# Reordering the tail of a graph network's first layer: masks, joins, degrees and a weight split moved to earlier places on each engine

## The reference

```python
h = relu(layernorm(x)); x = x + L0(h)   # mean over incoming edges @ W_l.T + b_l + h @ W_r.T, relu
h = relu(layernorm(x)); x = x + L1(h)   # transformer: 4 blocks, attention over the edges,
                                        # layer norms scaled by a conditioning vector of each node
h = relu(layernorm(x)); x = x + L2(h)   # weighted graph convolution, one weight for each edge
h = relu(layernorm(x)); x = x + L3(h)   # edge network: mish(mish(edge_feat @ W1) @ W2), summed to nodes
```

```python
ph = noise_levels * freqs
emb = concatenate([sin(ph), cos(ph)])
cond = silu(emb @ f_w1 + f_b1) @ f_w2 + f_b2
scale, bias = cond @ sw + sb, cond @ bw + bb
```

## Time and profile before

| | us |
|---|---|
| median of 3 runs | 1599.44 (1599.12 to 1599.72) |
| profiled execution, its own time | 1600.61 |
| span of the profiled execution | 1597.4 |
| PE busy | 1511.4 (95%) |
| DVE busy | 1187.2 (74%) |
| ACT busy | 1076.7 (67%) |
| POOL busy | 649.0 (41%) |

### The profile page before, as it was taken

How to read it: one execution, slowest core, us unless ns; L and a number is a source line. 1 busy time by engine, 2 the same in 40 slices (tenths; PEclk the granted TensorE clock), 3 DMA queues, 4 the chain that set the end, 5 groups by cost and what they waited for, 6 DMA issues and landing times. The chain is left out here.

```text
span 1597.4 us, 26151 instructions
## 1 busy us (share of the span) xinstructions
PE 1511.4 (95%) x9086; PEld 1216.4 (76%) x9086; DVE 1187.2 (74%) x2049; ACT 1076.7 (67%) x1557; POOL 649.0 (41%) x471
## 2 busy tenths in 40 slices
PE   4998899999999999999999999999999999999987
PEld 4765587778787878787864578888888888888874
DVE  8995647564656465646634399999999999999967
ACT  8844536543654465445532289999999999999953
POOL 3430200110012001200300677888888888888501
PEclk9999899999999999999999999999999999999989
DMA  3002320013002300120104777777777777777610
GB/s 110 1 2 87 93 86 27 7 51 116 27 7 61 105 27 7 54 93 27 69 27 140 178 158 151 154 157 151 157 151 158 153 157 153 157 154 155 159 34 33
DMA packets 88590, 151.47 MB, mean 95 GB/s; under 512 B 23611, under 2 KB 28603, under 8 KB 88003
## 3 DMA queue, kind: packets, MB, share of 16 engines
q0 software_dynamic: 54400, 85.33, 27.2%
q1 hardware_dynamic: 34114, 65.15, 12.7%
HBM read 141.02 MB, written 9.31 MB: 94 GB/s over the span
## 5 line engine op out<-in xcount | busy, mean ns | idle before, releaser
L1876 POOL DMA_INDIRECT edge_gathered<-dst_table,edge_index x158 | 272.1, 1722 | 59.1 <-issue 37.2
L227 PE MATMUL edge_z2p<-edge_w_hi,edge_h_hi 128*128 128x512 f32 x628 | 252.3, 402 | 0.6 <-DVE edge_late L2243 0.6
L227 PE MATMUL edge_z2p<-edge_w_hi,edge_h_lo 128*128 128x512 f32 x628 | 247.9, 395 | 0.0
L227 PE MATMUL edge_z2p<-edge_w_lo,edge_h_hi 128*128 128x512 f32 x628 | 247.6, 394 | 0.0
L1848 POOL DMA_INDIRECT edge_gathered<-src_table,edge_index x158 | 175.1, 1108 | 83.8 <-issue 79.8
L1079 POOL TENSOR_TENSOR h<-h,tr_row_b 128x512 f32<-128x512 f32 x40 | 59.2, 1513 | 271.5 <-ACT C L1325 271.1
L1068 POOL TENSOR_TENSOR tr_cw<-w_c,tr_cw 32x1024 fp32r<-32x1024 f32 x7 | 16.6, 2372 | 318.8 <-ACT tr_cw L1285 318.8
L227 PEld LDWEIGHTS edge_z2p<-edge_w_hi,edge_h_hi 128*128 128x128 f32 x628 | 118.3, 188 | 32.5 <-issue 7.7
L227 PEld LDWEIGHTS edge_z2p<-edge_w_hi,edge_h_lo 128*128 128x128 f32 x628 | 118.2, 188 | 27.9
L227 PEld LDWEIGHTS edge_z2p<-edge_w_lo,edge_h_hi 128*128 128x128 f32 x628 | 118.3, 188 | 24.2
L1095 PE MATMUL tr_one<-tr_yT_hi,tr_w_hi 128*128 128x256 f32 (+2 forms) x384 | 119.3, 311 | 4.2 <-issue 4.2
(11 more groups left out here) (380 smaller groups left out, 3964.5 us busy)
## 6 DMA issues: line engine op xcount, KB each, us to landing
w_c<-in_attr_T SPq DMA_DIRECT2D x78, 128.0 KB
w_a<-in_wv SPq DMA_DIRECT2D x4, 1024.0 KB, 5.4
w_b<-in_wq SPq DMA_DIRECT2D x4, 1024.0 KB, 5.2
w_a<-in_wk SPq DMA_DIRECT2D x4, 1024.0 KB, 7.5
w_b<-in_wo SPq DMA_DIRECT2D x4, 1024.0 KB, 6.9
w_a<-in_m SPq DMA_DIRECT2D x4, 1024.0 KB, 5.2
w_b<-in_m SPq DMA_DIRECT2D x4, 1024.0 KB, 5.3
w_c<-in_cond_w SPq DMA_DIRECT2D x4, 768.0 KB, 5.5
```

What stands on the lines that cost most here:

```text
L227: mm = pe.matmul(out, a, b, start=(n == 0), stop=(n == last))
L1876: pool.indirect_dma_start(out=from_rows[ring][:, j, :].bitcast(F32), out_offset=None, in_=k.dst_table, in_offset=bass.IndirectOffsetOnAxis ...
```

## The change

In the tail of `front` the same work is put in another order, and one piece of the transformer's start is moved into it. On PE, `degT` goes from behind the two `cond` products to behind the fifth aggregate (`AGG` is indexed by `AHEAD` = 4). In the ring `beside` it then has the bank of the first `hidden`, and the two `cond` products come after it. On VectorE, the five joins and the first four masks go ahead of the taking of `hidden`, the fifth mask behind it, and the reciprocal of the degrees ahead of `cond`. On ACT, four sums of counts and four aggregates come ahead of the exponential. The first half of the weight split is made at the end of this tail, into a tile `first_parts` that lives through the whole program; the edge layer uses the same bytes as the first of its two `h1_lo` tiles. `ph` and `turns` become names for other tiles.

```diff
+        plan.add(("agg",) + AGG[AHEAD], "sca")
+        plan.add(("degT", 0), "vec", "beside")
+        for m, f in AGG[AHEAD + 1:]:
             plan.add(("agg", m, f), "sca")
         for f in range(2):
             plan.add(("cond", f), "vec", "beside")
-        plan.add(("degT", 0), "vec", "beside")
...
-                for i in range(2):
+                for i in range(AHEAD):
+                    if i >= 2:
+                        act.wait_ge(has_ready, i - 1)
                     sum_counts(i)
...
+                    take_agg(*AGG[i])
+                act.wait_ge(cz_ready, 2)
+                act.activation(ce[:, :], cz[:, :], ACT.Exp, scale=-1.0).then_inc(ce_ready, 1)
+                act.wait_ge(has_ready, NT - 2)
+                sum_counts(NT - 1)
+                take_agg(*AGG[AHEAD])
                 for i in range(NT):
                     scale_W(i)
...
                 act.activation(k.dis[:, :], k.dis[:, :], ACT.Exp, scale=-0.5).then_inc(logs_ready, 1)
+                act.wait_ge(k.cw_loaded, 16)
+                act.activation(k.cw_first, k.w_c[0:CROWS, 0:2, :], ACT.Copy).then_inc(logs_ready, 1)
...
+                for i in range(NT):
+                    sum_W(i)
+                for i in range(NT - 1):
+                    no_edge(i)
                 for f in range(2):
                     bank = plan.take(dve, ("hidden", f))
...
+                no_edge(NT - 1)
                 dve.wait_ge(ce_ready, 1)
...
                 dve.wait_ge(logs_ready, NT + 1)
                 own(dve.tensor_tensor(k.dis[:, :], k.dis[:, :], k.has[:, :], ALU.mult))
+                dve.wait_ge(logs_ready, NT + 2)
+                rest = slice(PART, 2 * PART)
+                own(dve.tensor_tensor(k.cw_first[rest, :, :], k.w_c[rest, 0:2, :], k.cw_first[rest, :, :].bitcast(F32),
+                                      ALU.subtract))
...
-        cw_raw, cw = k.w_c[0:CROWS, :, :], sb("cw", [CROWS, 4, D], F32R)
+        cw_raw, cw = k.w_c[0:CROWS, :, :], [k.cw_first, sb("cw", [CROWS, 2, D], F32R)]
...
-                cut(0, 0)
+                act.sem_inc(cw_high, 1)
...
-                dve.wait_ge(cw_high, 1)
-                rest = slice(PART, 2 * PART)
-                dve.tensor_tensor(cw[rest, 0:2, :], cw_raw[rest, 0:2, :], cw[rest, 0:2, :].bitcast(F32),
-                                  ALU.subtract).then_inc(cw_ready, 1)
+                dve.sem_inc(cw_ready, 1)
                 scaled(0, 0, 0)
...
-        h1_hi, h1_lo = ([sb(f"{n}{a}", [P, KF, EDGE], F32R) for a in range(2)] for n in ("h1_hi", "h1_lo"))
+        h1_hi = [sb(f"h1_hi{a}", [P, KF, EDGE], F32R) for a in range(2)]
+        h1_lo = [cols(k.first_parts[:, :, :].rearrange("p a b -> p (a b)"), EDGE), sb("h1_lo1", [P, KF, EDGE], F32R)]
```

More of the change, by code:

```diff
@@ L608, in _ @@
                     plan.made(pe.matmul(bank[0:COND, 0:HALF], f1[:, :], emb[:, f * HALF:(f + 1) * HALF], start=True, stop=True))
-                for m, f in AGG[AHEAD:]:
-                    aggregate(m, f)
-                pe.wait_ge(silu_ready, 1)
-                for f in range(2):
-                    bank = plan.open(pe, ("cond", f))
-                    plan.made(pe.matmul(bank[0:CROWS, 0:HALF], f2[:, :], cz[:, f * HALF:(f + 1) * HALF], start=True, stop=True))
+                aggregate(*AGG[AHEAD])
                 bank = plan.open(pe, ("degT", 0))
@@ L620, in _ @@
                 plan.made(mm)
+                for m, f in AGG[AHEAD + 1:]:
+                    aggregate(m, f)
+                pe.wait_ge(silu_ready, 1)
+                for f in range(2):
+                    bank = plan.open(pe, ("cond", f))
+                    plan.made(pe.matmul(bank[0:CROWS, 0:HALF], f2[:, :], cz[:, f * HALF:(f + 1) * HALF], start=True, stop=True))
                 for i in range(NT):
@@ L769, in _ @@
                     dve.tensor_scalar(k.logc[:, i, :], sums[:, i, 0, 0:NP], 1.0, None, ALU.max).then_inc(maxed, 1)
-                for f in range(2):
-                    bank = plan.take(dve, ("hidden", f))
-                    ins = dve.tensor_scalar(cz[:, f * HALF:(f + 1) * HALF], bank[0:COND, 0:HALF], fb1[:, 0:1], None, ALU.add)
-                    plan.took(("hidden", f), ins)
-                plan.need(dve, ("hidden", 1))
-                dve.sem_inc(cz_ready, 2)
                 def sum_W(i):
@@ L791, in _ @@
                 dve.tensor_tensor(cz[:, :], cz[:, :], ce[:, :], ALU.mult).then_inc(silu_ready, 1)
-                for i in range(3, NT):
-                    sum_W(i)
+                bank = plan.take(dve, ("degT", 0))
+                plan.took(("degT", 0), dve.tensor_scalar(k.rdeg[:, :], bank[:, 0:NT], 1.0, None, ALU.max))
+                plan.need(dve, ("degT", 0))
+                step(dve.reciprocal(k.rdeg[:, :], k.rdeg[:, :]))
                 dve.wait_ge(has_ready, NT)
@@ L804, in _ @@
                 plan.need(dve, ("cond", 1))
-                bank = plan.take(dve, ("degT", 0))
-                plan.took(("degT", 0), dve.tensor_scalar(k.rdeg[:, :], bank[:, 0:NT], 1.0, None, ALU.max))
-                plan.need(dve, ("degT", 0))
-                step(dve.reciprocal(k.rdeg[:, :], k.rdeg[:, :]))
                 step(dve.tensor_copy(k.condT[:, :], cond_rows[:, :]))
@@ L1123, in scale @@
                     plan.open(pe, ("norm", b, s, i))
[L1124 removed]
+                    plan.made(pe.matmul(plan.at[("scale", b, s, i)].bank, k.condT[:, i * P:(i + 1) * P], cw[s][:, 0, :],
                                         start=True, stop=True))
```

36 lines of the change are left out of this document (17 added, 19 removed).

## The result

The changed kernel takes **1587.66 us** (median of 4 runs, 1587.03 to 1588.90) against 1599.28 for the kernel before in the same comparison: ratio 0.993, 95% interval 0.9918 to 0.9943, that is 9.1 to 13.1 us less. The forecast was 1590.3 (1588.0 to 1593.5) and faster. The profiled execution took 1587.25 us, its span 1585.3.

What follows compares the result with a forecast made beforehand. TensorE's stop before `degT`, caused by VectorE's late masks, and the half clock behind it bound the tail: 7.9 us, plus 1.2 for the weight split, makes 9.1; 1600.61 to 1591.5, median 1.17 lower: 1590.3 us (1588.0 to 1593.5).

Steps and rivals of the forecast that it cites:

- The stop before `degT`: Tail of `front`: TensorE idles 4.94 us until VectorE, late at its masks, frees a bank; removing this gains 7.9 us.
- its three terms: Of the 7.9 us: 4.94 of idle time, 1.0 of `degT`, 2.0 of half clock in the first left tile.
- The tie before the first left product: Three chains end near 146.9 us in the tail; VectorE's moved subtraction ends at 146.7, so 0.2 us are spare.
- VectorE's filled time: Five joins and four masks, 9.1 us, fill VectorE's 9.10 us of idle time; 2.7 us late at `hidden` is bearable.
- the lock: VectorE and GpSimd share a port pair; GpSimd's two additions, 2.50 us, would make VectorE 2.5 us late at `hidden`.
- joins longer than 0.77: Sign expected in the changed profile: VectorE's joins next to GpSimd's additions take longer than 0.77 us.
- The weight split: Transformer's start: with the subtraction moved into the tail, the first scale product follows the statistics directly, 1.2 us gained.
- the two steps: The stop before `degT`, 7.9 us, and the weight split, 1.2 us.
- rival C: Transformer's first value products, 4.05 us at half clock: an earlier or later rise gains or loses 2.0; gain's chance 0.12.
- The sum: 7.9 + 1.2 = 9.1 us less than the profiled execution, span 1597.4 to 1588.3; chance 0.60.
- P: Theory of the experiments: the gain beyond the sum belongs to the change, above all the split; 11 to 12.5 us altogether.

Runs made afterwards that it cites:

- e9: Kernel before plus five additional products, results unread, between `cond` and `degT`, filling TensorE's stop; 1595.91 us, ratio 0.9977.
- e1: Kernel before with only VectorE's order of joins and masks changed; 1592.53 us, ratio 0.9956.
- e10: The change with `degT` and its taking put back behind `cond`; 1589.70 us, ratio 0.9945.
- e2: Kernel before with only `degT` moved (plan, TensorE, reciprocal on VectorE), joins and masks as before; 1593.57 us, ratio 0.9964.
- e11: The change with GpSimd's last two additions of the bias held until VectorE has taken `hidden`; 1589.27 us, ratio 0.9946.
- e8: The change with eight small additional VectorE instructions ahead of the taking of `hidden`; 1594.83 us, 6.9 above the change.
- e3: Kernel before with only the weight split moved into the tail, with its tile; 1595.64 us, ratio 0.9982.
- e6: The change with the first half of the weight split put back into the transformer's start; 1589.88 us, ratio 0.9944.
- e5: The change again, unchanged, on the chip of e6 to e8; 1587.97 us (5 runs), ratio 0.9937 against the kernel before.
- e12: The change with e7's additional products except the five behind the left products; 1589.72 us, ratio 0.9944.
- e4: The change with five additional TensorE products, results unread, behind the left products; 1588.85 us, ratio 0.9933.
- e7: The change with unread products behind the left products, ahead of the first scale product and behind the first three transposed tiles; 1584.33 us, ratio 0.9912.

## Why the prediction was right, step by step

*The stop before `degT`, 7.9 us.* Right, with its three terms: the idle time went from 4.94 to 0, `degT` from 2.29 to 1.27 (taken as 1.2), and the first left product was taken at 146.88 (forecast 146.9). e9 separates stop and clock, 4.9 and 3.0. What the prediction put first, the move of `degT`, is not needed for it: in the traces the reordering of VectorE alone gives the same (e1, e10), and `degT` alone less (e2). The cause was named rightly, VectorE at its masks; the remedy needs only the order.

*The tie before the first left product.* The subtraction ended at 146.6 (forecast 146.7), ScalarE's copy at 145.0 (145.3). The forecast 0.2 us of slack is 0.27.

*VectorE's filled time and the lock.* The forecast said that VectorE would be late by 2.5 us at `hidden` through joins lengthened by GpSimd. The lock cost it 2.0, and in another way. The joins were running when GpSimd's additions came, and these waited: 5.02 us where 2.50 was the time alone. Then GpSimd went ahead, and two of the instructions behind the joins took 2.0 us longer together (1.78 and 1.55, less 0.83 and 0.48). The marker "joins longer than 0.77" failed; the price was nearly right. This is what the Trainium skill says in SBUF — State Buffer, section "SBUF: two separate sides": whichever of the two engines starts first holds the port pair for a whole instruction, and the other one waits. I had applied that rule with GpSimd as the one in front. e11 shows the lock by moving it. Of slack before TensorE feels VectorE's delay the forecast left 0.2 us; there are 1.2 (e8).

*The weight split, 1.2 us.* The subtraction left the transformer's start (the wait of the scale product is 6.50 instead of 7.87), 1.25 in e3, 1.36 between e6 and e5, and between e6 and e11 (168.18 and 166.73, less 0.09 for the loop). The mechanism was right.

*What was mis-sized* is the total: 11.6 instead of 9.1. In the profiled pair the two steps give 9.06. What lies beyond is half clock that one execution met and the other one didn't: 1.2 us gained among the first value products, which is the prediction's rival C, given 0.12 as a case of its own; 1.6 lost in the transformer and 1.5 gained at the start of the edge layer, on which the prediction says nothing; and with them the shorter wait for gathered rows, 1.0. The sum put all of this at nothing. How long the value products ran at half clock, from their start to the rise, differs from trace to trace: 4.05 before, 1.5 in the change, 1.9 in e5, 1.9 in e6, 2.7 in e11, 3.7 in e8. e11 has TensorE's tail of the change, to the 0.34 us of the loop, and still 1.2 us more of half clock here. The Trainium skill, TensorE: Matmul & The Clock Gate, Part 1, on which C was built, says that the moment of the rise isn't tied to the program's own start; these six agree, above all the change, e5 and e11, whose TensorE does the same work. The half clock at the start of the edge layer stands in the traces of before, e1, e3, e6, e8 and e12, and is missing in those of the change, e2, e4, e5, e7, e9, e10 and e11. The one in the transformer stands in the traces of the change, e2, e3, e4, e6, e8, e9, e10 and e11, and is missing in those of before, e1, e5, e7 and e12. Neither goes with one part of the change, and in the second the change and e5, two executions of one kernel, differ.

*Does the excess belong to the change?* Three measurements of kernels whose TensorE runs alike gave 11.6, 11.35 and 9.6 us (the change, e5, e11). Their intervals all reach to 9.1, the first one with its edge. Executions of one kernel lie 1.7 to 6.1 us apart here, and the traces of kernels with the same tail differ in such stretches. Yet each of the nine timed executions of the change itself (the result and e5) lies more than 9.1 us, by 9.4 to 12.3, below the median of the kernel before beside it, so for this kernel the excess came back. So 9.1 us are shown with their causes, in the traces; of the other 0.5 to 2.5 us the cause stays open, and how much is a lasting property of the earlier start and how much the luck of the executions that were timed. P, in the form that the split carries it, is neither shown nor excluded: e6 and e3 put the split at 1.9 and 3.0 by the medians; the intervals of e6 and e5 overlap, and that of e3, 1.4 to 4.3, begins just above the 1.3 of the traces.

## What to carry to other kernels

When TensorE waits for a bank, look at what the engine that must free it does first, and whether that work could have run in an idle stretch of its own earlier; reordering that one engine can do, as here up to the scale product, what reordering both does. Price a TensorE stop twice, by its length and by the half clock behind it (here 4.9 and 3.0 us), and test the two apart by filling the stop with products that nobody reads. Such filling gained 3.6 us here (e7's executions all lie below those of e5), but only where it covered the stop and the thin stretch behind it; half of it gained nothing.

## What the runs showed of the hardware that was not expected

- Two GpSimd additions of 128x512, 2.50 us with VectorE idle, took 5.02 when five VectorE joins with two operands in SBUF were already running, and 3.08 when they came between other instructions of VectorE. The joins themselves weren't lengthened (0.75 each).
- The two VectorE instructions that fell beside those additions lost about 1.0 us each, whichever they were: an addition of two tiles and an instruction with a single tile as input alike (1.78 and 1.55 in the change, 1.86 and 1.55 in e11).
- The granted clock fell to 0.54 in a stretch in which TensorE was busy for 7.47 of 7.50 us; ahead of it lay 4.46 us of additional products and then 3.6 us with 1.04 us of work (e4). It held at 1.00 in the same place when products stood in those 3.6 us and between the turned tiles too (e7).
